# Rotary queries in two product groups instead of three, with the swap of features by transfers inside SBUF and the sums on POOL

## What is computed

```python
def _rotate_half(x):
    x1 = x[..., ::2]
    x2 = x[..., 1::2]
    return jnp.stack((-x2, x1), axis=-1).reshape(x.shape)
def _apply_rope(x, cos, sin):
    return x * cos + _rotate_half(x) * sin
q = _rms_norm(x @ w_qa, q_a_norm_w) @ w_qb        # 96 wide, then 16 heads of 128 + 64
q_nope, q_rope = (q[..., :D_NOPE], q[..., D_NOPE:])
q_rope = _apply_rope(q_rope, cos, sin)
k_rope = _apply_rope(k_rope[:, None], cos, sin)
scores = jnp.einsum('bhsd,bhtd->bhst', q_full, k_full) * scale
attn = jax.nn.softmax(jnp.where(mask[None, None], scores, jnp.finfo(scores.dtype).min), axis=-1)
out = jnp.einsum('bhst,bhtd->bhsd', attn, v)
```

## Time and profile before

| | |
|---|---|
| three runs, us | 1254.86, 1255.21, 1247.85; median 1254.86 |
| the profiled execution's time | 1254.86 us |
| its span, first to last instruction | 1253.1 us |
| mean granted TensorE clock | 0.956 of full speed |
| busy share: PE, DVE, ACT, POOL | 91%, 68%, 63%, 55% |

### The profile page before, as it was taken

One profiled execution on the slowest core, in us unless ns is written; L12 is line 12 of the kernel. 1 busy time (PEld: TensorE's weight loads), 2 busy tenths in 40 slices (PEclk: granted clock), 3 DMA queues, 4 the chain that ended last, 5 costly groups with the idle time before them and its releaser, 6 DMA issues. The chain is left out here.

```text
span 1253.1 us, 27841 instructions
## 1 busy us (share of the span) xinstructions
PE 1146.3 (91%) x11372; PEld 958.8 (77%) x11372; DVE 846.8 (68%) x1900; ACT 787.5 (63%) x1166; POOL 690.3 (55%) x569
## 2 busy tenths in 40 slices
PE   2856899999999999999999999999999778989897
PEld 1744577888888888888888888888887667888886
DVE  2632876677676776777777677776675576767676
ACT  1254577777777878777787787877777532322222
POOL 0022366777777768686787776877777711202000
PEclk9876699999999999999999999999999879989998
DMA  9301110000100200100020020010000310000000
GB/s 277 95 1 48 29 44 18 2 18 25 38 19 2 62 2 19 44 19 19 2 62 18 2 61 2 19 44 19 18 2 1 114 57 1 1 18 1 18 18 17
DMA packets 57695, 39.91 MB, mean 32 GB/s; under 512 B 7744, under 2 KB 57152, under 8 KB 57408
## 3 DMA queue, kind: packets, MB, share of 16 engines
q1 hardware_dynamic: 51216, 33.94, 9.2%
q10 hardware_dynamic: 6352, 4.19, 1.4%
HBM read 33.66 MB, written 4.46 MB: 30 GB/s over the span
## 5 line engine op out<-in xcount | busy, mean ns | idle before, releaser
L669 POOL TENSOR_TENSOR pt_lo<-pt 128x1024 f16<-128x1024 f32 x192 | 370.5, 1939 | 181.5 <-ACT pt L726 181.2
L782 DVE TENSOR_REDUCE gates<-bank 128x1 f32<-128x512 f32 x384 | 261.6, 689 | 148.0 <-PE bank L849 145.1
L717 ACT ACTIVATE pair<-shift 128x1024 f32<-128x1024 f32 x256 | 263.7, 1030 | 12.2 <-ACT pt L730 0.4
L726 ACT ACTIVATE pt<-pair 128x1024 f32<-128x1024 f32 x192 | 196.2, 1022 | 108.3 <-PE pair L876 107.7
L891 PEld LDWEIGHTS bank<-values,pt 128*128 128x128 bf16 x2176 | 196.8, 98 | 80.1 <-issue 52.6
L891 PE MATMUL bank<-values,pt 128*128 128x65 f16 x2176 | 235.2, 194 | 6.0 <-DVE lat L808 5.1
L893 PE MATMUL bank<-values,pt 128*128 128x64 f16 x2176 | 231.8, 192 | 0.0
L895 PE MATMUL bank<-values,pt_lo 128*128 128x65 f16 x2176 | 230.8, 194 | 0.0
L675 POOL TENSOR_TENSOR pt_lo<-pt 128x512 f16<-128x512 f32 (+3 forms) x256 | 178.3, 722 | 45.0 <-ACT pt L730 44.9
L893 PEld LDWEIGHTS bank<-values,pt 128*128 128x128 bf16 x2176 | 202.0, 98 | 0.0
L895 PEld LDWEIGHTS bank<-values,pt_lo 128*128 128x128 f16 x2176 | 201.3, 97 | 0.0
(11 more groups left out here) (218 smaller groups left out, 2380.0 us busy)
## 6 DMA issues: line engine op xcount, KB each, us to landing
turn_by<-rope_cos_by_feature SPq DMA_DIRECT2D x64, 128.0 KB, 3.0
turn_by<-rope_sin_by_feature SPq DMA_DIRECT2D x64, 128.0 KB, 3.0
xs<-in_L_attn_x ACTq DMA_DIRECT2D x1, 2048.0 KB, 25.5
lat<-in_L_attn_w_o SPq DMA_DIRECT2D x1, 2048.0 KB, 26.6
xs_again<-in_L_attn_x SPq DMA_DIRECT2D x1, 2048.0 KB, 8.1
out<-xs_again SPq DMA_DIRECT2D x4, 512.0 KB, 2.8
lat<-in_L_wmod SPq DMA_DIRECT2D x1, 1536.0 KB, 16.3
lat<-in_L_attn_w_qb SPq DMA_DIRECT2D x1, 1152.0 KB, 8.0
```

The lines of the kernel that those rows point to most:

```text
L669: pool.tensor_tensor(out=pt_lo[:, at].rearrange("p a n -> p (a n)"), in0=full, in1=cut(full), op=ALU.subtract).then_inc(low_ok, 1)
L717: act.activation(s_pair[u % 2][:, :, :], shift[:, item % SHIFTS:item % SHIFTS + 1, :].to_broadcast([P, 2, BW]), ACT.Copy).then_inc(seeded[ ...
L726: act.activation(pt[:, at], s_pair[u % 2][:, :, :], ACT.Exp).then_inc(exp_done, 1)
L782: dve.tensor_reduce(out=to, in_=of, axis=AXX, op=ALU.max).then_inc(work_seen["v"], 1)
```

## The change

Per pair, two groups of products are left. Part 0 makes the rotary features of both heads in one bank: head 1's in partitions 0 to 63, head 0's in 64 to 127, each with its 32 even features ahead of its 32 odd ones. DVE multiplies the bank by the signed sine into a new tile `by_sin`, and the two halves by the cosine into `qf`. SP then issues four transfers of 32 partitions from `by_sin` to `swapped`, which exchange even and odd. Part 1 makes the latent features of both heads; ACT copies both. In the round of part 2 POOL adds `swapped` to `qf` (twice). In the round of part 3 ACT makes `q_hi` and POOL `q_lo`, a round later than before. The tables arrive in eight transfers of 32 partitions in place of four of 64, SP's order is the next pair's loads and then this pair's swap, the weights kept in DRAM are a third smaller, and the keys' rotary features are written in the same order of even and odd.

```diff
 def seen_by(n):
-    return {"max": "v", "shift": "a", "q": "va"}[use[0]] if use[0] != "q" or use[2] < 2 else ""
+    return {"max": {"v": 1}, "shift": {"a": 1}, "q": {"v": 3} if use[-1] == 0 else {"a": 2}}[use[0]]
...
-        for at, hd in ((KVL, 0), (P, 1)):
-            moves += [(at, 0, even[:, :, hd], 1.0), (at, 1, odd[:, :, hd], 1.0)]
-        for at, hd in ((2 * P, 1), (2 * P + DR, 0)):
-            moves += [(at, 0, odd[:, :, hd], -1.0), (at, 1, even[:, :, hd], 1.0)]
+        moves = [(at + e * (DR // 2), turned[:, :, hd, e]) for at, hd in ((0, 1), (DR, 0)) for e in range(2)]
...
+                def loads(p):
+                    hp, g = PAIRS[p]
+                    if p == 0 or hp != PAIRS[p - 1][0]:
                         if p > 0:
-                            sp.wait_ge(work_done, WORK[("q", p - 1, 2)] + 1)
+                            sp.wait_ge(work_done, WORK[("q", p - 1, 1)] + 1)
                         for part in range(2):
                             sp.dma_start(wq[part][:, :].bitcast(F32), wq_dram[part, hp]).then_inc(wq_in, 16)
                     if p > 1:
-                        sp.wait_ge(q_sum, 2 * p - 2)
+                        wait_seen(sp, WORK[("q", p - 2, 0)])
                     for n, name in enumerate(("cos_t", "sin_t")):
...
+                            for e in range(2):
+                                at = half * DR + e * (DR // 2)
+                                sp.dma_start(turn_by[at:at + DR // 2, p % 2, n, :].rearrange("d (j p) -> d j p", j=BT),
+                                             of[(e + n) % 2]).then_inc(turn_in[p % 2], 16)
+                def swap(p):
+                    wait_seen(sp, WORK[("q", p, 0)])
+                    if p > 0:
+                        sp.wait_ge(q_sum, 2 * p)
+                    for at in range(0, P, DR // 2):
+                        sp.dma_start(swapped[at:at + DR // 2, :], by_sin[at ^ (DR // 2):(at ^ (DR // 2)) + DR // 2, :]).then_inc(q_swapped, 16)
+                loads(0)
+                for p in range(len(PAIRS)):
+                    if p + 1 < len(PAIRS):
+                        loads(p + 1)
+                    swap(p)
...
+                def query_sum(p, r):
+                    if r >= 0:
+                        pool.wait_ge(low_ok, OPS[r + 1])
+                    pool.wait_ge(q_swapped, 64 * p + 64)
+                    for hd in range(2):
+                        pool.tensor_tensor(out=qf[ROT[hd], hd, :], in0=swapped[ROT[hd], :], in1=qf[ROT[hd], hd, :],
+                                           op=ALU.add).then_inc(q_sum, 1)
+                        pool.wait_ge(q_sum, 2 * p + hd + 1)
...
-                    p, part = PREP_AT.get(r, (0, 3))
+                    p, part = PREP_AT.get(r, (0, 4))
                     if part == 2:
+                        query_sum(p, r)
+                    if part == 3:
                         query_low(p)
...
                 def query_high(p):
                     if p >= Q_SLOTS:
                         act.wait_ge(s_done, 2 * FIRST_UNIT[2 * (p - Q_SLOTS) + 2])
+                    wait_seen(act, WORK[("q", p, 1)])
+                    act.wait_ge(q_sum, 2 * p + 2)
                     for hd in range(2):
-                        act.wait_ge(q_sum, 2 * p + hd + 1)
...
+                def query_turn(p):
+                    n = WORK[("q", p, 0)]
+                    if p > 0:
+                        dve.wait_ge(q_lo_ok, 2 * p)
+                        dve.wait_ge(q_swapped, 64 * p)
...
+                    dve.wait_ge(work_done, n + 1)
+                    dve.scalar_tensor_tensor(out=by_sin[:, :], in0=work_of(n)[:, :], scalar=sign[:, :], in1=turn_by[:, p % 2, 1, :],
+                                             op0=ALU.mult, op1=ALU.mult).then_inc(work_seen["v"], 1)
+                    for hd in range(2):
+                        dve.tensor_tensor(out=qf[ROT[hd], hd, :], in0=work_of(n)[ROT[hd], :], in1=turn_by[ROT[hd], p % 2, 0, :],
                                           op=ALU.mult).then_inc(work_seen["v"], 1)
```

More of the change, by code:

```diff
@@ L101 @@
     WORK_ORDER += [("shift", SHIFT_AT[_r])] if _r in SHIFT_AT else []
-    WORK_ORDER += [("q", *PREP_AT[_r])] if _r in PREP_AT and PREP_AT[_r][1] < 3 else []
+    WORK_ORDER += [("q", *PREP_AT[_r])] if _r in PREP_AT and PREP_AT[_r][1] < 2 else []
 WORK = {w: n for n, w in enumerate(WORK_ORDER)}
@@ L200, in prepare @@
         wv_t = sb(own, "wv_t", [P, H, KVL])
-        wq_hi = sb(own, "wq_hi", [QL, NP, 3 * P], F32R)
-        wq_lo = sb(own, "wq_lo", [QL, NP, 3 * P], F32R)
+        wq_hi = sb(own, "wq_hi", [QL, NP, 2 * P], F32R)
+        wq_lo = sb(own, "wq_lo", [QL, NP, 2 * P], F32R)
         ccol = sb(own, "ccol", [P, KD])
@@ L340, in _ @@
                 act.wait_ge(wscaled, 2)
-                for at, e, of, sgn in moves:
-                    act.activation(pair_cols(wq_hi, at, e), of, ACT.Copy, scale=sgn).then_inc(wqh_ok, 1)
+                for at, of in moves:
+                    act.activation(half_cols(wq_hi, at), of, ACT.Copy).then_inc(wqh_ok, 1)
                 for g in range(2):
@@ L584, in attend @@
     with ExitStack() as own:
-        wq = [sb(own, f"wq_pair_{p}", [QL, 3 * P], F32R) for p in ("hi", "lo")]
+        wq = [sb(own, f"wq_pair_{p}", [QL, 2 * P], F32R) for p in ("hi", "lo")]
         turn_by = sb(own, "turn_by", [P, 2, 2, BW])
@@ L589, in attend @@
         qf = sb(own, "qf", [P, 2, BW])
+        by_sin = sb(own, "by_sin", [P, BW])
+        swapped = sb(own, "swapped", [P, BW])
+        sign = sb(own, "sign", [P, 1])
         pt = sb(own, "pt", [P, PT_RING, 2, BW])
@@ L600, in attend @@
         q_sum = sem("q_sum")
-        q_turned = sem("q_turned")
+        q_swapped = sem("q_swapped")
+        sign_ok = sem("sign_ok")
         q_hi_ok = sem("q_hi_ok")
@@ L617, in wait_seen @@
         def wait_seen(eng, n):
-            use = WORK_ORDER[n]
-            if use[0] == "q" and use[2] == 2:
-                eng.wait_ge(q_sum, 2 * use[1] + 2)
             for e in seen_by(n):
@@ L686, in _, with query_plain @@
             def _(act):
-                def query_plain(p, part):
-                    n = WORK[("q", p, part)]
-                    if part == 0 and p > 0:
+                def query_plain(p):
+                    n = WORK[("q", p, 1)]
+                    if p > 0:
                         act.wait_ge(q_lo_ok, 2 * p)
                     act.wait_ge(work_done, n + 1)
-                    act.activation(qf[PLAIN[part], part, :], work_of(n)[PLAIN[part], :], ACT.Copy).then_inc(work_seen["a"], 1)
+                    for hd in range(2):
+                        act.activation(qf[PLAIN[hd], hd, :], work_of(n)[PLAIN[hd], :], ACT.Copy).then_inc(work_seen["a"], 1)
                 def query_high(p):
@@ L739, in _ @@
                         seed(r + 2)
-                    p, part = PREP_AT.get(r, (0, 3))
-                    if part < 2:
-                        query_plain(p, part)
-                    if part == 2:
+                    p, part = PREP_AT.get(r, (0, 4))
+                    if part == 1:
+                        query_plain(p)
+                    if part == 3:
                         query_high(p)
@@ L809, in evacuate @@
                                     o_bank[:, 0:BT * (KVL + 1)].rearrange("p (t n) -> p t n", t=BT)).then_inc(o_seen, 1)
+                dve.memset(sign[:, :], 1.0).then_inc(sign_ok, 1)
+                dve.wait_ge(sign_ok, 1)
+                for at in (DR // 2, DR + DR // 2):
+                    dve.memset(sign[at:at + DR // 2, :], -1.0).then_inc(sign_ok, 1)
                 for r in ROUNDS:
@@ L816, in _ @@
                     p, part = PREP_AT.get(r, (0, 4))
-                    if part < 3:
-                        query_turn(p, part)
+                    if part == 0:
+                        query_turn(p)
                     if 0 <= r + 2 < NU and seed_on_vector(r + 2):
@@ L911, in _ @@
                     p, part = PREP_AT.get(r, (0, 3))
-                    if part < 3:
+                    if part < 2:
                         query_products(p, part)
```

68 lines of the change are left out of this document (22 added, 46 removed).

## The result

The changed kernel takes 1380.75 us (median of 4 runs, 1378.82 to 1388.98); the kernel before, on the same chip, 1254.6 us (1247.85 to 1255.21). The ratio is 1.1027, 95% interval 1.0989 to 1.1065: 10% slower, against a forecast of 1332 us and a range to 1362. The profiled execution has a span of 1379.5 us, 126.4 more than before.

A forecast was written before the change was run, and what follows sets the result against it. PE was taken to bound the attention. Start +6, pairs 3 and 4 +1.3 and +1.6, six rounds of four pairs +66, pairs 29 to 31 +2.2: +77 on 1254.86 gives 1332 us, range 1282 to 1362.

The forecast's parts named there:

- the close places: Six steady places with pairs 4 rounds apart: late swap makes PE go on 5.8 us later, plus 0.4 and 1.3.
- What bounds the kernel: Attention: PE, busy 99.93 of 100 us, sets the pace, so any new wait lengthens the time in full.
- rival (b): POOL's sums cost half, 1.45 us for two: 1297 us; chance 0.17, shared with a swap that is hidden.
- The ordinary pair: Sums and q_lo on POOL delay weigh: 1.2 to 1.5 us lost per pair without the bank wait, 1.8 with it.
- the bank wait: PE at part 1 waits for DVE's three products of part 0 to free the bank: 0.3 to 0.5 us, pairs 4 to 28.
- 1.1 for four swaps: Close place, SP's queue: the swap's four issues take 1.1 us, behind the next pair's loads.
- 0.4 each: Close place, SP's queue: eight half-size table loads at 0.4 us per issue, bounds 0.3 and 0.6.
- Landing 2.3 us: Close place: the swap lands 2.3 us after its issues, as for the weights, at 418.5.
- Rival (c): Clock falls to half after each of six stops, 5 us each: 1332 + 30 = 1362 us; chance 0.18.
- Pair 3: Pair 3, just behind the start, taken at +1.3 us in the sum.
- The start: First pairs with nothing to hide their chain: 7.7 us later, less PE's group and DVE's sums, taken as 6.
- rival (a): Sums and swap fit in POOL's idle time, PE's 22 us less bank waits of 10 remain: 1243 us; chance 0.07.

The follow-up runs named there:

- e2: Changed kernel with POOL's two sums over 256 of the 512 columns, half the rotary sum left out; 1352.34 us.
- e8: Kernel before, with one matmul in place of three in its third group (products with a low part left out); 1244.62 us against 1255.38.
- e1: Changed kernel with SP issuing the swap of a pair ahead of the next pair's loads; 1356.93 us.
- e3: Changed kernel with a second copy of the fp32 query qf and two slots of shifts fewer; 1341.92 us.
- e15: e14 with a second slot of the fp32 query qf; 1265.68 us.
- e6: e5 with q_hi on ACT and q_lo on POOL back in the round of part 2; 1321.69 us.
- e13: Changed kernel, pairs 8 rounds apart and started two rounds earlier, q_hi and q_lo five rounds after first products, swap ahead of loads; 1268.93 us.
- e4: Changed kernel with the two sums on DVE in the round of part 2, none on POOL; 1331.6 us.
- e5: e4 with the swap issued ahead of the next pair's loads, as in e1; 1297.61 us.
- e7: e6 with part 0's products and DVE's turning first in their round; 1306.74 us.
- e14: Changed kernel: sums on DVE, swap first, part 0 first, pairs 8 rounds apart, started two earlier, q_hi and q_lo five rounds after first products; 1262.64 us.
- e16: Control: kernel before with pairs 8 rounds apart, prepared two rounds earlier, high and low parts two rounds later; 1262.11 us.
- e9: Changed kernel with pairs prepared at least 8 rounds apart instead of 4; 1363.95 us.

## Why the prediction was wrong

Direction and mechanism held, and the sizes of the waits failed; the time lies 19 us outside the range. The step that failed is the term of the close places: 7.5 us each in the sum, 12.7 in the mean of the trace, because the swap's four issues were priced at 1.1 us and took 2.4, one issue ahead of them ran long, and the lower clock behind the stop was left out of the sum.

**What bounds the kernel: right.** PE has no slack in the attention, so each wait went into the time in full. e2 shows it at a rate of one to one, and e8 the other way, with 10.8 us gained of 15.

**The sums on POOL: right.** Forecast 1.28 us each at full price for half the partitions. The trace has a mean of 1316 ns:

```profile
L680 POOL TENSOR_TENSOR q_lo<-qf,q_hi 128x512 fp32r<-128x512 f32 x64 | 86.4, 1371 | 1.7 <-ACT q_hi L722 1.7
L673 POOL TENSOR_TENSOR qf<-swapped,qf 64x512 f32<-64x512 f32 x64 | 84.2, 1316 | 52.9 <-DMA swapped<-by_sin 48.6
```

So 64 partitions cost what 128 do, and rival (b), half price, fell; e2, with half the columns, is what it takes to get 734 ns. By the rule of the Trainium skill (GPSIMD Engine Reference, section 2), that each core has its own 16 partitions, the two sums were to cost the full price; the trace agrees, with 2.64 us for pair 10 and 2.59 for pair 11.

**The ordinary pair: mechanism right, 1.8 against 2.5.** The course for pair 10 came out instruction by instruction. Two of its durations were too small: the `q_lo` pair takes 2.98 us, not 2.55, since one of the two now runs beside DVE's L805 (2.48 at the close place, where DVE stands still), and the low part of unit 88 ends 0.7 us late, the bank wait (0.4) among it. Over twelve pairs that is 9 us.

**The close place: the step that failed.** The prediction had PE going on 5.8 us later than before, and 0.4 for the bank wait of pair 11. PE stood 9.2 us and went on 9.3 us later: the distance to the kernel before was 43.1 us ahead of pairs 11 and 12, and at this query product it is 474.27 - 421.88 = 52.4. The terms:

- "1.1 for four swaps": they took 2.42 us. Line L652 (ns per issue, min/median/max, then landing):

```profile
L652 SPq DMA_DIRECT2D swapped<-by_sin x128: 507/591/1802, 122.1 to 1085.2; - x128
...
DMA to landing us min/median/max: 1.9/2.0/4.0
```

An issue cost 0.59 us. I had a row for issues, 0.61 and 0.43 us, and used neither of them for the swap: 0.27 each was taken from nothing.
- "0.4 each" for eight tables, 3.4 us in the sum: seven of them took 0.43 us each, as taken, and the eighth 1.92, so that they took 5.3 us together. Each of the other five places has such a long issue ahead of the swap too, of 0.9 to 1.5 us. The upper bound, 0.6 each, would have covered most of it. What makes an issue long is open.
- Landing 2.3 us, put behind the end of the last issue. The row counts from an issue's start: the last swap was issued from 462.87 to 463.46 and had landed at 464.85, 2.0 us after its start and 1.4 after its end. This term was 0.9 us too long and hid part of the other two. The Trainium skill (DMA: Bandwidth & Descriptors, the anatomy of one DMA) has about 2.15 us by its rule, an estimate for 64 KB from a fit to transfers that POOL issues; counted from the issue's start, the trace agrees within 0.15 us for these of SP.
- So POOL could start on the swap 10.1 us after SP's first load, not 7.6, and it waited 4.6 us, not 1.8. At the six places the swap landed 9.2 to 10.0 us after the first load. The rest of the chain (2.6, 1.9, 2.5, 2.2 us) came as forecast.
- The clock. Rival (c) was right that it falls behind such a stop, and wrong in its price: 5 us per place was taken, and what rows show is 0.7 us in the three products (1.44 us to 475.71 against 0.70 in the earlier trace rows) and 2.0 us from there to the weigh of unit 104, of which 0.4 is a longer wait of that weigh for DVE's L821. It should have been a term of the sum, not a rival at 0.18: in the earlier trace rows the granted clock was 0.50 behind a stretch in which PE had stood as long.

At this place 9.3 of delay, 0.7 and 2.0 behind it and 1.6 for pair 12's own course make 13.7 us, against 5.8 + 0.4 + 1.3. Over the six places the term was short by 5.2 us in the mean: 31 us of the 49 that are missing.

**Pair 3: a place overlooked.** It was priced as an ordinary pair, 1.3 us, and cost 7.7. Its swap stands behind the loads too; e1 takes it to 1.1.

**The start: 6 against 10.8.** The chain of pair 0 was forecast to end at 132 and ended at 132.1, by luck: DVE had the tables 0.6 us earlier than forecast, and issues and landing of the swap took 0.5 longer. Item 2's first chunk, forecast at 141.6, came at 142.54. Then I took 1.7 us off for work saved, and stopped there, while the chain repeats for pair 2. e3 shows that a part of it is the single buffer: with a second one 10.8 is 6.3 (and in e15 15.2 is 10.6).

**Experts: 0 against -5.4.** From the last weigh to the end the kernel before takes 263.4 us at a granted clock of 0.91, the changed one 257.9 us at 0.95. The traces of the other kernels fall into the same two groups: 263.3 to 264.7 us at 0.91 (e2, e6, e8 to e13, e15), and 257.7 to 258.3 us at 0.94 to 0.95 (e3, e4, e5, e7, e14, e16); e1 lies between. None of them touches the experts. So the 5.4 us go with the clock there, and two kernels of the list can differ by some 6 us for this alone. What sends an execution to the one or the other was not tested.

**The signs named beforehand.** Right: sums near 1.28 us, weigh waiting up to 1.8 us for `pt_lo`, 192 L854 rows. Right in kind and too small in size: PE busy 86 and not 90, L780 waiting 9.0 us and not 4, the swap there after 10.1 us and not 7.5. The clock under 1.00 in the steady window (0.97), the sign of (c), came as well, beside the forecast and not in its place.

**"POOL has room after all", rival (a): wrong for this schedule, right for the engine.** e13 keeps the sums on POOL and costs 1.8 us in all over pairs 5 to 28. What it turned on was not the sums' length alone, as the prediction has it, but the distance between POOL's two pieces of work and the place of the swap in SP's queue.

## What to carry to other kernels

When work is moved to an engine that is a quarter idle, price it by the gap between two deadlines in its queue, not by its share: here 5.6 us of added and moved work within two rounds cost 2.5 us each time, and the same work three rounds apart 0.0 to 0.7. A chain through a transfer is as long as the queue in front of it, so count every issue at the measured price of its own kind and put the transfer that others wait for first. And before a grouping is judged, give both groupings the same placement: here placement and the order of SP's transfers took the 10% down to 1.1% with the sums still on POOL (e13). With the sums on DVE and almost the same placement for both, the grouping's own balance was zero, and the kernel before, as it stood, is still 0.7% faster than either.

## What the runs showed of the hardware that was not expected

- DVE and POOL slow each other when the DVE instruction has both inputs in SBUF: e6's sums took 682 ns at least and 3.09 us for two beside `pt_lo`, while L772 and L769, each with an input in a PSUM bank, kept means of 689 and 749 ns. The Trainium skill (SBUF — State Buffer, Who interferes with whom) speaks of a port pair that the two engines share and lock, for a DVE instruction with two SBUF inputs beside a POOL one that reads SBUF; these rows agree. It goes the other way too: in the changed kernel 36 of POOL's `q_lo` ran beside no such DVE instruction and took 1.26 to 1.30 us, 28 ran beside DVE's L805 and took 1.27 to 1.76.
- Issues on SP are not constant: of some 400 in the attention of the changed kernel 13 took 0.9 to 1.9 us, where most of their kinds take 0.31 to 0.60. The kernel before has one such among 144.
- A stop of TensorE of 8 to 9 us had around and behind it 10 to 14 us at 1.2 GHz, stops of 4.1 to 5.4 us (e1, e9) 3.4 to 6.8 us of it, and e13, whose steady stretch has none, stays at a granted clock of 1.00 in it.
